# Taking the forward transforms of a cross-attention apart once more, into products with 128 rows

## What is computed

```python
q = (queries @ Wq.T + bq).reshape(B, L, H, dk)
k = (keys @ Wk.T + bk).reshape(B, L, H, dk)
v = (values @ Wv.T + bv).reshape(B, L, H, dk)
qf = jnp.fft.rfft(q, axis=1)
kf = jnp.fft.rfft(k, axis=1)
corr = jnp.fft.irfft(qf * jnp.conj(kf), n=L, axis=1).mean(axis=-1)
weights, delays = jax.lax.top_k(corr, topk)      # topk = 6
w = jax.nn.softmax(weights, axis=-1)
# each head's v, shifted round by its six delays and summed with these weights, then @ Wo.T + bo
```

## Time and profile before

| | |
|---|---|
| median of 3 runs | 699.96 us (698.32 to 700.57) |
| the profiled execution's own time | 700.49 us |
| its span in the profile | 698.7 us |
| PE busy, share of the span | 84% |
| DVE, ACT, POOL busy | 65%, 41%, 17% |
| mean granted clock of PE | 0.943 of full speed |

### The profile page before, as it was taken

How to read it: one execution, slowest core, us unless ns; L and a number is a source line. 1 busy time by engine, 2 the same in 40 slices (tenths; PEclk the granted TensorE clock), 3 DMA queues, 4 the chain that set the end, 5 groups by cost and what they waited for, 6 DMA issues and landing times. The chain is left out here.

```text
span 698.7 us, 16972 instructions
## 1 busy us (share of the span) xinstructions
PE 585.3 (84%) x7448; PEld 425.6 (61%) x7448; DVE 455.8 (65%) x890; ACT 283.2 (41%) x518; POOL 117.4 (17%) x102
## 2 busy tenths in 40 slices
PE   4868679999999999897696876599999758998984
PEld 2545467777768677776443445488887654555542
DVE  2972557767685777774728799563276764676664
ACT  1874633433443344333344353333323154544441
POOL 1001350160042006000101213444000020000000
PEclk9999899999999999998799998899999887999998
DMA  5501420240042003113410005200000000000001
GB/s 173 211 1 31 151 94 3 70 146 3 4 152 63 4 32 123 37 61 113 160 31 30 31 2 193 96 1 0 1 1 0 1 0 1 1 0 31 31 6 56
DMA packets 26537, 37.51 MB, mean 54 GB/s; under 512 B 4641, under 2 KB 13602, under 8 KB 26463
## 3 DMA queue, kind: packets, MB, share of 16 engines
q1 hardware_dynamic: 26463, 36.42, 15.8%
HBM read 34.31 MB, written 2.10 MB: 52 GB/s over the span
## 5 line engine op out<-in xcount | busy, mean ns | idle before, releaser
L298 DVE SCALAR_TENSOR_TENSOR arena<-bank,conv_w,arena 128x511 f32<-128x511 f32 (+2 forms) x72 | 53.1, 746 | 31.3 <-ACT arena L1079 15.7
L1461 POOL COPY arena<-v_win 128x256 f32<-128x256 f32 x32 | 20.1, 651 | 178.0 <-PE bank L736 177.9
L1911 ACT COPY arena<-bank 128x512 f32<-128x512 f32 x40 | 23.3, 585 | 56.9 <-PE bank L1714 36.7
L1714 PE MATMUL bank<-v_win,arena 128*128 128x256 f32 x192 | 45.6, 386 | 0.0
L2486 PE MATMUL bank<-v_win,arena 128*128 128x256 bf16 x288 | 36.5, 279 | 7.9 <-DVE arena L2573 6.9
L736 PE MATMUL bank<-arena 128*32 128x128 f32 x512 | 35.7, 409 | 6.7 <-ACT arena L1090 6.2
L1140 ACT COPY arena<-bank 128x512 f32<-128x512 f32 x40 | 21.5, 590 | 46.7 <-PE bank L858 46.7
L1714 PEld LDWEIGHTS bank<-v_win,arena 128*128 128x128 f32 x192 | 37.0, 194 | 5.5 <-issue 0.4
L2476 PE MATMUL bank<-arena,v_win 128*128 128x512 bf16 x144 | 36.4, 390 | 2.8 <-DVE arena L2544 2.8
L2486 PEld LDWEIGHTS bank<-v_win,arena 128*128 128x128 bf16 x288 | 28.4, 100 | 16.7 <-DVE arena L2573 7.9
L1095 ACT COPY arena<-bank 128x256 f32<-128x256 f32 x32 | 19.3, 602 | 46.4 <-PE bank L749 46.3
(11 more groups left out here) (275 smaller groups left out, 1355.1 us busy)
## 6 DMA issues: line engine op xcount, KB each, us to landing
arena<-in_toep_w SPq DMA_DIRECT2D x32, 256.0 KB, 2.9
arena<-in_toep_l SPq DMA_DIRECT2D x32, 256.0 KB, 3.5
arena<-in_xT SPq DMA_DIRECT2D x12, 512.0 KB, 4.3
arena<-in_x SPq DMA_DIRECT2D x4, 512.0 KB, 3.8
arena<-in_ctx SPq DMA_DIRECT2D x4, 512.0 KB, 4.3
out<-arena SPq DMA_DIRECT2D x4, 512.0 KB, 2.9
qkv_w<-in_qkv_wT SPq DMA_DIRECT2D x1, 768.0 KB, 5.6
v_win<-in_w_gateT SPq DMA_DIRECT2D x1, 768.0 KB, 4.7
```

Of the source, the lines that this page charges most:

```text
L298: return nc.vector.scalar_tensor_tensor(out=acc[:, j:L], in0=src[:, 0:L - j], scalar=conv_w[:, m, CONV_K - 1 - j:CONV_K - j], in1=acc[:, j:L],
L1714: i = mm(oo, src[:, k, f * P:(f + 1) * P], w[:, k, :], start=(k == 0), stop=(k == KT - 1 and f > 0))
L1911: nc.scalar.copy(dst(i), bank[RING_FIRST + n % RING].rearrange("p (t c) -> p t c", c=dst(i).shape[-1]))\
```

## The change

A second level of taking apart is put in, for even and odd frequencies in different ways.

- **Even frequencies.** `sums` and `ctx_sums` write the sum of the halves, then the sum and the difference of its own halves (256 columns each) into the first part, and last the difference of the halves over the second part. There are four operations with three points at which one waits for another, where there were two independent ones. Frequencies that leave no remainder by four need the one tile of 128 rows, those that leave two the other.
- **Odd frequencies.** The second tile of 128 rows is mirrored by a matmul with a permutation matrix (`mirror_x`, `mirror_ctx`, one product of 128x128 by 128x256) into bank 7 or 6, and DVE (`fold_odd`) makes two combinations of the first tile and the mirrored rows, by two operations with one operand in the bank, the second waiting for the first.
- **The forward transform.** `forward` has four products for each 128 channels, each with 128 rows and 128 moving columns, none of which accumulate; two write every second column of the bank. So there are still 16 instructions for a sequence and kind, with half the columns.
- **The order.** On PE `mirror_ctx(0)` and `mirror_x(1)` stand ahead of `turn_o(3)`, and `forward_ctx(0)` stands behind it. On DVE `fold_x(0)` stands between `softmax_after(3)` and `head_norm(2)`, `fold_ctx(0)` and `fold_x(1)` between `shift(2)` and `head_norm(3)`, and `sums(2)` ahead of `products(0)`.
- **The constants.** Three more arrays are loaded in stage 4 behind the rows of sequence 1, over constants that stages before it have done with. `dft` stays for the delays.

```diff
-const = {n: sb("c_" + n, [P, w]) for n, w in const_shapes.items()}
+ident = sb("c_ident", [P, P])
+of_rule = sb("of_rule", [P, sum(w for w, in const_shapes.values())])
+const = carve(of_rule, const_shapes)
...
+folds = carve(of_rule, {n: (w,) for n, w in FOLD_CONST.items()})
...
+for n in FOLD_CONST:
+    sp.dma_start(folds[n], dr["c_" + n]).then_inc(late_loaded.sem, 16)
...
 def forward(b, kind, src):
     for d in range(KT):
         o = spectrum_bank(b, kind, d)
-        for par in range(2):
-            for k in range(2):
-                i = mm(o[:, par * 256:(par + 1) * 256], src[:, par, k, d * P:(d + 1) * P],
-                       dft[:, k, par * 256:(par + 1) * 256], start=(k == 0), stop=(k == 1))
+        evens = o[:, 0:256].rearrange("p (ri h two) -> p ri h two", ri=2, two=2)
+        for g, dst in enumerate((evens[:, :, :, 0], evens[:, :, :, 1], o[:, 256:384], o[:, 384:512])):
+            i = mm(dst, src[:, g // 2, g % 2, d * P:(d + 1) * P],
+                   fold[:, g, :].rearrange("p (ri h) -> p ri h", ri=2) if g < 2 else fold[:, g, :],
+                   start=True, stop=True)
         i.then_inc(s4["spec_mm"].sem, 1)
+def mirror_x(b):
+    pe.wait_ge(s4["xeo"].sem, s4["xeo"].at(b, 4))
+    if b:
+        pe.wait_ge(s4["x_fold"].sem, s4["x_fold"].at(b - 1, 2))
+    mm(bank[XREV_BANK][:, 0:D], mirror, xeo_of(b)[:, 1, 1, :], start=True, stop=True).then_inc(s4["x_rev"].sem, 1)
...
 def forward_x(b):
-    pe.wait_ge(s4["xeo"].sem, s4["xeo"].at(b, 2))
+    pe.wait_ge(s4["x_fold"].sem, s4["x_fold"].at(b, 2))
...
 (PE's order)
+mirror_x(0)
 forward_x(0)
...
+mirror_ctx(0)
+mirror_x(1)
+turn_o(B - 1)
 forward_ctx(0)
-turn_o(B - 1)
 project_q(0)
 project(B - 1)
 project_k(0)
+mirror_ctx(1)
 project_v(0)
 forward_x(1)
+mirror_x(2)
 forward_ctx(1)
 project_q(1)
+mirror_ctx(2)
 project_k(1)
 project_v(1)
 forward_x(2)
+mirror_x(3)
 forward_ctx(2)
+mirror_ctx(3)
 project_q(2)
 correlation(0)
...
 (DVE)
-v.tensor_tensor(xeo_of(b)[:, 0, :, :], x1[:, 0:2, :], x1[:, 2:4, :], ALU.add).then_inc(s4["xeo"].sem, 1)
-v.tensor_tensor(xeo_of(b)[:, 1, :, :], x1[:, 0:2, :], x1[:, 2:4, :], ALU.subtract).then_inc(s4["xeo"].sem, 1)
+v.tensor_tensor(eo[:, 1, :, :], x1[:, 0:2, :], x1[:, 2:4, :], ALU.add).then_inc(s4["xeo"].sem, 1)
+dve.wait_ge(s4["xeo"].sem, s4["xeo"].at(b, 1))
+v.tensor_tensor(eo[:, 0, 0, :], eo[:, 1, 0, :], eo[:, 1, 1, :], ALU.add).then_inc(s4["xeo"].sem, 1)
+v.tensor_tensor(eo[:, 0, 1, :], eo[:, 1, 0, :], eo[:, 1, 1, :], ALU.subtract).then_inc(s4["xeo"].sem, 1)
+dve.wait_ge(s4["xeo"].sem, s4["xeo"].at(b, 3))
+v.tensor_tensor(eo[:, 1, :, :], x1[:, 0:2, :], x1[:, 2:4, :], ALU.subtract).then_inc(s4["xeo"].sem, 1)
+def fold_odd(b, eo, rev_bank, reversed_, done):
+    dve.wait_ge(reversed_.sem, reversed_.at(b, 1))
+    odd, rev = eo[:, 1, :, :], bank[rev_bank][:, 0:D]
+    v.scalar_tensor_tensor(out=odd[:, 1, :], in0=odd[:, 0, :], scalar=but_first[:, 1:2], in1=rev,
+                           op0=ALU.mult, op1=ALU.add).then_inc(done.sem, 1)
+    dve.wait_ge(done.sem, done.at(b, 1))
+    v.scalar_tensor_tensor(out=odd[:, 0, :], in0=rev, scalar=but_first[:, 0:1], in1=odd[:, 0, :],
+                           op0=ALU.mult, op1=ALU.add).then_inc(done.sem, 1)
...
 shift(b - 1)
+if b == B - 1:
+    fold_ctx(0)
+    fold_x(1)
 if b == B - 2:
     sums(0)
 if b < B - 1:
     softmax_after(b + 1)
+if b == B - 2:
+    fold_x(0)
 head_norm(b)
...
+sums(2)
 products(0)
-sums(2)
+fold_ctx(1)
+fold_x(2)
 products(1)
+fold_ctx(2)
+sums(3)
 coefficients(0)
-sums(3)
+fold_x(3)
+fold_ctx(3)
 best(0)
```

More of the change, by code:

```diff
@@ L83, in shape_constants @@
     c["dft"] = dft.reshape(2, P, 4 * P).transpose(1, 0, 2).reshape(P, -1)
+    fold = np.zeros((P, 4, P))
+    for q in range(2):
+        fold[:, q, 0:P // 2], fold[:, q, P // 2:P] = dft[0:P, 0, q::2], dft[0:P, 1, q::2]
+    fold[:, 2], fold[:, 3] = dft[0:P, 2], dft[0:P, 3]
+    fold[0, 3] = dft[P, 3]
+    c["fold"] = fold.reshape(P, -1)
+    c["mirror"] = ((i[:, None] + i[None, :]) % P == 0)
+    c["but_first"] = np.where(i[:, None] > 0, [[-1.0, 1.0]], 0.0)
     c["idft"] = inv.reshape(P, -1)
@@ L93 @@
 LATE_CONST = ("dft", "idft", "not_dc", "is_dc", "dc_row")
+FOLD_CONST = {"fold": 4 * P, "mirror": P, "but_first": 2}
 class Signal:
@@ L188, in layer @@
         arena = sb("arena", [P, 30624])
-        const_shapes = {n: a.shape[1] for n, a in shape_constants().items() if n not in LATE_CONST}
-        const = {n: sb("c_" + n, [P, w]) for n, w in const_shapes.items()}
-        ident = const["ident"]
-        levels = const["levels"][:, :].rearrange("p (k c) -> p k c", k=LEVELS - 1)
+        const_shapes = {n: (a.shape[1],) for n, a in shape_constants().items()
+                        if n not in LATE_CONST and n not in FOLD_CONST and n != "ident"}
+        ident = sb("c_ident", [P, P])
+        of_rule = sb("of_rule", [P, sum(w for w, in const_shapes.values())])
+        const = carve(of_rule, const_shapes)
+        levels = const["levels"].rearrange("p (k c) -> p k c", k=LEVELS - 1)
+        folds = carve(of_rule, {n: (w,) for n, w in FOLD_CONST.items()})
+        fold, mirror, but_first = folds["fold"].rearrange("p (g c) -> p g c", g=4), folds["mirror"], folds["but_first"]
         late = carve(v_win[:, :, :, :].rearrange("p two t c -> p (two t c)"), {
@@ L322, in _ @@
                 for n in const:
-                    if n != "ident":
-                        load(const[n][:], dr["c_" + n])
+                    load(const[n], dr["c_" + n])
                 sp.wait_ge(s1["pads"].sem, PADS)
@@ L1570, in layer @@
         CORR_BANK, TURN4_BANK = 6, 7
+        XREV_BANK, CREV_BANK = 7, 6
         ot_bank, y4_bank = (lambda b, i: bank[(0, 2, 2, 0)[b] + i]), (lambda b, i: bank[(4, 0, 4, 2)[b] + i])
@@ L1693, in forward, with mirror_ctx @@
                         o = spectrum_bank(b, kind, d)
-                        for par in range(2):
-                            for k in range(2):
-                                i = mm(o[:, par * 256:(par + 1) * 256], src[:, par, k, d * P:(d + 1) * P],
-                                       dft[:, k, par * 256:(par + 1) * 256], start=(k == 0), stop=(k == 1))
-                        i.then_inc(s4["spec_mm"].sem, 1)
+                        evens = o[:, 0:256].rearrange("p (ri h two) -> p ri h two", ri=2, two=2)
[3 more added lines that the diff above has]
+                                   start=True, stop=True)
+                        i.then_inc(s4["spec_mm"].sem, 1)
+                def mirror_x(b):
[3 more added lines that the diff above has]
+                    mm(bank[XREV_BANK][:, 0:D], mirror, xeo_of(b)[:, 1, 1, :], start=True, stop=True).then_inc(s4["x_rev"].sem, 1)
+                def mirror_ctx(b):
+                    pe.wait_ge(s4["ceo"].sem, s4["ceo"].at(b, 4))
+                    if b:
+                        pe.wait_ge(s4["c_fold"].sem, s4["c_fold"].at(b - 1, 2))
+                    else:
+                        pe.wait_ge(s3["st_out"].sem, s3["st_out"].at(B - 1, 1))
+                    mm(bank[CREV_BANK][:, 0:D], mirror, ceo_of(b)[:, 1, 1, :], start=True, stop=True).then_inc(s4["c_rev"].sem, 1)
                 def forward_x(b):
-                    pe.wait_ge(s4["xeo"].sem, s4["xeo"].at(b, 2))
+                    pe.wait_ge(s4["x_fold"].sem, s4["x_fold"].at(b, 2))
                     forward(b, "x", xeo_of(b))
                 def forward_ctx(b):
-                    pe.wait_ge(s4["ceo"].sem, s4["ceo"].at(b, 2))
+                    pe.wait_ge(s4["c_fold"].sem, s4["c_fold"].at(b, 2))
                     forward(b, "c", ceo_of(b))
@@ L1746, in turn_delays @@
                         pe.wait_ge(s4["af"].sem, s4["af"].at(p - 1, 5))
+                    else:
+                        pe.wait_ge(s4["x_fold"].sem, s4["x_fold"].at(B - 1, 2))
                     for k in range(4):
@@ L1811, in _ @@
                     if b == B - 2:
-                        pe.wait_ge(late_loaded.sem, 16 * 5)
+                        pe.wait_ge(late_loaded.sem, 16 * (5 + len(FOLD_CONST)))
+                        mirror_x(0)
                         forward_x(0)
@@ L2175, in sums, with fold_x, fold_ctx @@
                     dve.wait_ge(s3["x1_out"].sem, s3["x1_out"].at(b, 4))
-                    x1 = x1_of(b)
-                    v.tensor_tensor(xeo_of(b)[:, 0, :, :], x1[:, 0:2, :], x1[:, 2:4, :], ALU.add).then_inc(s4["xeo"].sem, 1)
-                    v.tensor_tensor(xeo_of(b)[:, 1, :, :], x1[:, 0:2, :], x1[:, 2:4, :], ALU.subtract).then_inc(s4["xeo"].sem, 1)
+                    x1, eo = x1_of(b), xeo_of(b)
+                    v.tensor_tensor(eo[:, 1, :, :], x1[:, 0:2, :], x1[:, 2:4, :], ALU.add).then_inc(s4["xeo"].sem, 1)
[12 more added lines that the diff above has]
+                                           op0=ALU.mult, op1=ALU.add).then_inc(done.sem, 1)
+                def fold_x(b):
+                    fold_odd(b, xeo_of(b), XREV_BANK, s4["x_rev"], s4["x_fold"])
+                def fold_ctx(b):
```

(1 more changed line is left out.)

14 lines of the change are left out of this document (9 added, 5 removed).

## The result

The changed kernel took 715.34 us in the median of 4 runs (712.16 to 720.13), the kernel before 699.33 in the same job (4 runs, 698.32 to 700.57). The ratio is 1.0212, with a 95% interval from 1.0174 to 1.0251. A later job gave 713.36 us against 701.12, ratio 1.0184 (1.0138 to 1.0231). The ratios are worked out from fast runs alone and differ a little from the quotients of the medians. So it is slower, as forecast, but by 12 to 16 us and not by 5, and 715.34 lies above the range.

What follows compares the result with a forecast made beforehand. PE's unbroken stream, started by DVE, was taken to set the time; start +4.9, then -10.1 + 1.8 + 2.2 + 1.6 + 3.0 + 1.4, gave +4.8 us, a median of 704.8 us, range 699.5 to 709.0.

Steps and rivals of the forecast that it cites:

- The start: PE's stream, beginning at `turn_o(3)`, starts 4.9 us later because DVE's path to `head_norm(3)` grows.
- +0.4 for such meetings: Before `head_norm(3)`, DVE loses 0.4 us more to POOL's longer `ctx_sums`, between 0 and +1.3.
- The saving: Forward transforms in PE's stream: 0.110 us an instruction instead of 0.2156, six transforms saving 10.1 us.
- Rival 4: Forward transforms: 128-column products take 0.21 us each, limited by weight loads, so nothing is saved; 713 us, chance 0.05.
- The wait at `mirror_x(3)`: In PE's stream, the mirroring of x3 waits 3.0 us for DVE's `sums(3)`.
- the wait at `forward_ctx(1)`: In PE's stream, the forward transform of ctx1 waits 1.6 us for DVE's `fold_ctx(1)`, behind `sums(2)` and `products(0)`.
- The clock: PE's slow clock after the two new waits: 0.8 of one 1.7 us spell, +1.4 us, between 0 and 3.4.
- rival 3: Both stream waits and a longer idle stretch before it each cost a slow spell: +3.4 us more, 708.2, chance 0.13.
- The stream's sum: Length of PE's stream to `forward_delays(0)`: -10.1 + 1.8 + 2.2 + 1.6 + 3.0 + 1.4 us.
- The rule on the port: DVE and POOL share a port; folds, with one input in a bank, run beside POOL, otherwise `fold_ctx(1)` costs 2.2 us more.
- Rival 1: The stream's start is put off by 2.8 us instead of 4.9, without a cold spell: +1.3 us, 701.3, chance 0.15.
- rival 2: PE's stream has no waits, as DVE reaches the folds and `sums(3)` first: -1.2 us, 698.8, chance 0.12.

Runs made afterwards that it cites:

- e2: The changed kernel with `sums(3)` ahead of `products(1)` on DVE: 707.97 us, ratio 1.0091 to the kernel before.
- e1: The changed kernel with POOL waiting for `products(0)` before `with_bias(0)`: 713.08 us, ratio 1.0175 to the kernel before.
- e3: The changed kernel with `sums(2)` ahead of `residual(3)` on DVE: 707.93 us, ratio 1.0117 to the kernel before.
- e6: The changed kernel with sums and folds moved earlier or into DVE's wait, `mirror_x(1)` later, POOL's ctx2 sums earlier: 695.09 us, ratio 0.9916 to the kernel before.
- e9: Only even frequencies taken apart, on the kernel before, with `sums(1)`, `sums(2)` and POOL's ctx2 sums moved earlier or into DVE's wait: 692.08 us, ratio 0.9895.
- e11: e6 with `fold_ctx(0)` between `residual(2)` and `shift(2)`, `forward_ctx(0)` ahead of `turn_o(3)`, `mirror_x(1)` behind `project_q(0)`: 691.71 us, ratio 0.9880 to the kernel before.
- e8: The changed kernel without mirrors and folds, only even frequencies taken apart, the earlier PE and DVE order except `sums(3)`: 696.67 us, ratio 0.9937 to the kernel before.

## Why the prediction was wrong

The direction was right, and so were the later start and both waits, but the size was off by more than a factor of two. By the prediction's own steps:

- **The start**, +4.9 forecast, +5.7 found; `turn_o(3)` forecast near 452.4, found at 452.60. `sums(0)` and `fold_x(0)` cost 0.9 and 1.2, and the folds of ctx0 and x1 1.8, near their terms; the operation with a bank takes 0.48 where I took 0.415. `sums(1)` cost 2.4 and not 0.9, since two of its operations met POOL's longer sums; I had +0.4 for such meetings. These four come to 6.3; 0.5 came back in `weigh(3)`, which lost less to POOL than before (11.90 us against 12.43), and 0.1 in `head_norm(3)`.
- **The saving**, 0.110 us an instruction forecast, 0.112 found. Rival 4 falls, and with it the rule of the Trainium skill as I had drawn it on to these instructions (page TensorE: Matmul & The Clock Gate, section "Part 3: Packing small matmuls — row/col tiling"). The same section of the Trainium skill also lets a load go ahead into a background weight buffer, which I had left out.
- **The wait at `mirror_x(3)`**, 3.0 forecast, 2.88 found, and e2 shows it to be the order of `sums(3)`.
- **The step that failed: the wait at `forward_ctx(1)`**, "`products(0)` 4.73 (462.72 to 467.45)" and so "+1.6". PE was ready at 474.69 + 0.43 = 475.12 and went on at 480.96, 5.8 later. I took the duration of `products(0)` from a place where its multiplications end (465.21) just before `with_bias` begins (465.27), and used it 1.5 us further on, where they don't. So `products(0)` took 9.05 us and not 4.73; PE came when I had said, 10.2 us after the start of `residual(3)`'s last part (464.90 to 475.12). The row that says what happens there was in my hands: 2.84 us for one operation that met `with_bias`. I weighed it for the fold and not for the products, which have both inputs in SBUF. At that row's price two multiplications lose 4.3 us, and 1.6 + 4.3 gives 5.9, an estimate made afterwards. e1 and e3 show it from two sides: with the meeting taken away the multiplications are at 0.69, and the wait is 1.35 or none.
- **The clock**, 0.8 of a spell, +1.4. There were two, one behind each wait: (3.42 - 1.79) and (2.93 - 1.79), and 0.6 on the mirror ahead of the second, 3.4 in all. That is the upper bound I had given, and rival 3 in part, which had a spell behind each wait but priced them at 1.4 + 3.4. Behind the wait of 1.35 us in e1 there was none, so at least a part of the first spell seems to come with the length of the wait that was mis-sized; no run varied that length alone. The spell at the stream's start was there before too and cost about the same.

The stream's sum by the terms as found, with the second wait counted as the first is (498.26 to 501.30): -10.0 + 1.8 + 2.2 + 5.8 + 3.0 + 3.4 = +6.2, which is what the two profiles differ by. The forecast had -0.1. The medians differ by 16.0 us in the first job, 4.3 more than the two profiled executions, and by 12.2 in the second; what makes up the 4.3 stays open.

The rule on the port held where I had used it. The page SBUF — State Buffer, section "SBUF: two separate sides" of the Trainium skill, has DVE blocked by a running operation of POOL when both of its inputs are in SBUF. This trace agrees: the fold, with one input in a bank, took 0.48 at 449.00 while POOL's L2473 ran from 448.64 for 0.73 us, and `products(0)` was blocked. By that rule, applied to all that was moved, I would have seen the collision.

Rival 1 named a smaller start and rival 2 a stream without waits. Neither came for this order of work, but rival 2 is what e6, e9 and e11 are.

## What to carry to other kernels

When work is moved, take its duration from the place it moves to: look up what the other engines do in those microseconds, for every operation in the moved queue and not only for the new ones. A saving on the engine that bounds a stage is worth what the others leave of it; here 6 us of matmul time became 12 us of loss and, with the same operations moved within their queues, 8 to 9 us of gain, of which 2 are the slow spell that no longer falls on the stream. Before a second and costlier half of an idea is added, run the first half alone.

## What the runs showed of the hardware

- DVE operations with two inputs in SBUF wait out whole operations of POOL, even tiny ones: one of 128x64 took 2.37 us (`coefficients(0)`, at 501.43) beside an operation of `with_bias` that ran from 501.32 for 2.40. Operations with one input in a bank and reductions did not (0.47, 2.29).
- Waits of 2.88 and 5.68 us in a busy stream (and of 3.73 in e3 and 3.81 in e1) were each followed by slow instructions, in the changed kernel 0.183 to 0.214 us instead of 0.112. After 1.35 and 1.97 us (e1) and 1.74 (e9) the granted clock was 1.00; after 2.29 us it was once full and once not the earlier trace rows.
- A matmul that writes every second column of a bank is as fast as one that writes them all: sixteen instructions, half of them such, took 1.79 us, 0.112 each, and in e8, where they stand by themselves, four took 0.44 (465.95 to 466.39), 0.110 each, as in the earlier trace rows.
- The kernel before varied by 9.3 us over 18 of its 20 runs in one job and by 11.6 over all of them, together with its mean granted clock, 0.953 to 0.934. Differences of a few us between kernels need many runs, or the lengths of single stretches from the profile.
